# Relative attention of layer 1: scores as 64-row by 32-column tiles read straight from the projected keys, with four banks for scores and values and turn-back sharing two

## The chip, the cores and the metric

The kernel runs on 1 core of one Trainium2 chip. It is a whole vision-transformer tower in one program: 64 images, 26 tokens each (one class token and a 5 by 5 grid), width 192, four layers. The metric is the device time of one execution in microseconds (us); lower is better. All arithmetic is fp32; the large products are split into high and low fp32r parts, the small ones (scores, values) are plain fp32 matmuls, and the profiler records such a plain fp32 matmul as two MATMUL and two LDWEIGHTS instructions.

Engines are named as in the profile: PE is TensorE's matmul side, PEld its weight loads (which overlap PE), DVE is VectorE, ACT ScalarE, POOL GpSimd, SP SyncE.

## The reference, cut to what matters

Only the attention of layer 1 is touched. For every image, with 12 heads of 64 features:

```
qkv = (x @ qkv_w.T).reshape(b, n, 3, HEADS, HEAD_DIM).transpose(2, 0, 3, 1, 4)
q, k, v = (qkv[0], qkv[1], qkv[2])
attn = jnp.einsum('bhqd,bhkd->bhqk', q, k) * scale
r_p_k = tab_kv[iv] + tab_kh[ih]
attn = attn + jnp.einsum('bhqd,qkd->bhqk', q, r_p_k) * scale
attn = jax.nn.softmax(attn, axis=-1)
out = jnp.einsum('bhqk,bhkd->bhqd', attn, v)
r_p_v = tab_vv[iv] + tab_vh[ih]
out = out + jnp.einsum('bhqk,qkd->bhqd', attn, r_p_v)
out = out.transpose(0, 2, 1, 3).reshape(b, n, QKV_DIM)
return out @ proj_w.T + proj_b
```

`iv` and `ih` are the row and column distances of two tokens in the grid (a fixed index for the class token), so the relative parts are small products with tables of 10 rows each.

## The kernel before, in words

`attention(cfg, ...)` is one function for all attentions of the tower. For layer 1, `cfg.kind` is "rel", `G` is 2 and `NC` is 6: the 64 images are worked in 8 turns (`i` = 0 to 7) of 8 images, 208 tokens; each turn has two tiles (`g` = 0, 1; tile number `t` = 2i + g) of four images, each image in 32 partitions. q and k are projected transposed, six chunks each of 128 partitions (two heads of 64 features) by 208 tokens.

What runs in a turn is written out by hand as `order` (for PE and ACT) and `dve_order` (for DVE), lists of steps with the number of turns they run ahead: on PE k of the next turn, relative mass of tile 0 (`mass`), q of the next turn, `scores` 0 of the next turn, `values` 0, projection of v, `scores` 1, output projection of the turn before (`out`), mass 1, values 1, v, and turning the result back (`back`). The engines are held together by counting semaphores alone; each runs its list in order.

- Keys. ACT copies a projected chunk of k from PSUM to `k_t` (L1975). The chunk holds two heads one above the other, so `spread` (L2168 to L2179) has DVE multiply each chunk by a 0/1 mask per head into `k_x` (L2177), 12 instructions a turn, and raises `k_done`.
- Scores (`scores`, L1744). For tile t, 6 chunks by 4 images make 24 matmuls (L1775) of 128 rows by 32 stationary columns (the queries) and 52 moving columns (the masked keys of two heads), all into one bank, `bank[4 + g]`. PE waits for `s_used` (that tile t - 2 has been read), and on tile 0 of a turn for `k_done` and for the last copy of q. Behind them come 24 matmuls with the tables of the keys (`rel_scores`, L1785); ACT copies that result to `rel` (L2021), and DVE's `shift` starts with it (L2237, L2243), adds the scores (L2251, L2252), subtracts the maximum; ACT takes the exponential (L2028), DVE's `normalise` divides, sums the relative mass (L2290) and transposes the probabilities (L2299).
- Values (`values`, L1799). 48 recorded matmuls from the probabilities and v (L1806) and from the mass and the tables (L1832), into one of three banks 0 to 2 in turn; ACT copies them out (L2052, `av_used`).
- Back (`add_back`, L1898 and L2334). The output is turned back in pieces of 128 tokens (one or two a turn) into bank 3, by two transposes a piece (L1907, L1908); DVE adds each to the residual (L2338), and PE waits for that before the next piece. The five turns 1, 3, 4, 6 and 7 have two pieces.
- Banks 6 and 7 serve all other results in turn (`job`).

Of the kernel before, what the change touches and what calls it, by code (L numbers as in the profile page):

```python
# [18 lines left out]
ALU = mybir.AluOpType  # L19
# [81 lines left out]
def vit_tower(nc, a, out, stop=99):  # L101
# [12 lines left out]
    with ctx:  # L114
# [1340 lines left out]
        def attention(cfg, res, *others, stats_too=True):  # L1455
# [14 lines left out]
            rel_kind = cfg.kind == "rel"  # L1470

            kq = {"performer": [("fk", 0, 1)]}.get(cfg.kind, [("k", 0, 1), ("q", 0, 1)])
# [30 lines left out]
            else:  # L1503
# [33 lines left out]
            def added_back(i, g):  # L1537
# [7 lines left out]
            NA, NB = len(av_banks), len(back_banks)  # L1545

            def back_at(y, tiles):

                return bank[2][:, D * (y - tiles[0]):D * (y - tiles[0]) + D] if tiled else bank[back_banks[y % NB]]

# [4 lines left out]

            def score_banks():

                return psum[:, 3 * 512:6 * 512].rearrange("p (r x) -> p r x", r=3)[:, :, 0:NC * pairs * SLOT]

# [173 lines left out]
            def tensor(pe):  # L1733
# [10 lines left out]
                def scores(i, g):  # L1744
                    t = G * i + g
                    pe.wait_ge(s_free.sem, s_free_at + t - (0 if tiled else 1))
                    if g == 0 and cfg.kind == "causal" and i == 0:
                        keep_clock(bank[4], 8)
                    if cfg.mix and t == 0:
                        pe.wait_ge(mix["scores"], 1)  # L1750
                    if g == 0:
                        pe.wait_ge(s["k_done"].sem, b["k_done"] + i + 1)
                        used(last_qk[0], i, last_qk[1])
                    if tiled:
                        for c in range(NC):
                            kx = key_rows(i, c * pairs, pairs).rearrange("p (u n) -> p u n", n=n)
# [42 lines left out]
                def values(t, g):  # L1799
# [8 lines left out]
                    for v in range(halves):  # L1808

                        unit = halves * t + v  # L1810
                        pe.wait_ge(s["av_used"].sem, b["av_used"] + unit - NA + 1)
                        ob = bank[av_banks[unit % NA]]
                        if no == 2:
                            low_heads = H * 2 // 3
                            for c in range(2):
                                for y in range(in_cell):
                                    for strip in range(4):
                                        h = in_cell * strip + y if c == 0 else low_heads + in_cell * (strip % 2) + y
                                        ins = product(ob[:, 104 * c:104 * c + 104], h, strip, y == 0, y == in_cell - 1)
                        else:  # L1820
                            if v == 0:
                                pe.wait_ge(s["rel_table"].sem, b["rel_table"] + 5)
                                used("mass", t, 0)
                            for k in range(3):
                                c, p = divmod(3 * v + k, 2)
# [3 lines left out]
                                part = rel_mass[g][:, 128 * c:128 * c + 128].rearrange("p (b s) -> p b s", s=32)  # L1829
                                for u in range(2):  # L1830
                                    r0 = 128 * p + 64 * u
                                    ins = nc.tensor.matmul(o[64 * u:64 * u + 64, :], rel_table[:, r0:r0 + 64],  # L1832
                                                           part[:, :, 0:SLOT], start=False, stop=True)
# [64 lines left out]
                def add_back(i, g):  # L1898
                    used("out", i, 1)
                    ident = shp[:, SHAPE_COLS["ident"]]  # L1900
                    tiles = added_back(i, g)
                    for y in tiles:

# [42 lines left out]
            def scalar(act):  # L1946
# [7 lines left out]
                def projections(i, ys):  # L1954

                    if cfg.kind == "causal" and i:

                        act.wait_ge(s["qk_ready"].sem, b["qk_ready"] + 4 * (i - 1) + parts.index(ys) + 1)
                    elif cfg.kind != "performer":
                        act.wait_ge(s["k_done"].sem, b["k_done"] + i)  # L1960
# [59 lines left out]
                def rel_scores(t, g):  # L2020
                    nc.scalar.activation(rel[g][:, :, :].rearrange("p h r -> p (h r)"),  # L2021
                                         job("rel", t, 0)[:, 0:240], ACT.Identity)\
                        .then_inc(s["job_used"].sem, 1)
# [7 lines left out]
                def values(i, g):  # L2031
# [9 lines left out]
                    for v in range(halves):  # L2041
                        act.wait_ge(s["av_full"].sem, b["av_full"] + halves * t + v + 1)
                        src = bank[av_banks[(halves * t + v) % NA]][:, 0:104 * m].rearrange("p (c n) -> p c n", c=m)
                        dst = o4[:, v * m:v * m + m, g, :]
# [52 lines left out]
            def vector(dve):  # L2097
# [90 lines left out]
                def shift(t, g):  # L2188
# [3 lines left out]
                    if tiled:  # L2192
                        n4 = [128, 3, NC * pairs, SLOT]
                        sc = score_banks().rearrange("p r (h s) -> p r h s", s=SLOT)
                        z_as, mx_as = z.rearrange("p (r h) s -> p r h s", r=3), mx.rearrange("p (r h) -> p r h", r=3)
                        spread_out = mx_as.unsqueeze(3).to_broadcast(n4)
# [30 lines left out]
                    if cfg.kind == "rel":  # L2227
# [19 lines left out]
                        z4 = z[:, :, 1:SLOT].rearrange("p h (a c) -> p h a c", c=5)  # L2247
                        s4 = sc[:, :, 1:SLOT].rearrange("p h (a c) -> p h a c", c=5)
                        m0 = m12[:, 2, :].unsqueeze(2)
                        link(nc.vector.tensor_tensor(m0, rl[:, :, 0:1], rl[:, :, 10:11], ALU.add))  # L2250
                        nc.vector.tensor_tensor(z[:, :, 0:1], sc[:, :, 0:1], m0, ALU.add)  # L2251
# [5 lines left out]
                        src = z  # L2257
                    link(nc.vector.tensor_reduce(mx_as, src, AX.X, ALU.max))
# [113 lines left out]
            for name, uses in (("s_used", cfg.kind != "softmax"), ("z_full", cfg.kind in ("softmax", "rel", "causal")),  # L2372
                               ("p_full", cfg.kind != "performer"),
                               ("qk_ready", cfg.kind in ("performer", "causal"))):
                if not uses:
# [351 lines left out]
```

## Time and profile before

| | |
|---|---|
| time before, median of 3 runs | 2929.98 us (2927.67 to 2931.74) |
| the profiled execution | 2936.78 us, its span 2935.0 us |
| PE busy in the span | 2697.6 us, 92% |
| DVE busy | 2054.5 us, 70% |
| ACT busy | 1051.7 us, 36% |
| mean granted TensorE clock | 0.944 of full speed |
| the layer-1 attention | about 1645 to 1897 us of the span |

The shares are means over a program of very different stages; the layer-1 attention is under 9% of it. "idle before, releaser" tells how long an engine stood before an instruction and which instruction of another engine ended that; "issue" is a wait for nothing that the profile shows.

### The profile page before, as it was taken

How to read it: one execution, taken by the hardware profiler on the slowest of the kernel's cores; microseconds unless marked ns; L12 is line 12 of the kernel's file. 1: busy time of each engine (PE TensorE's matmuls, PEld its weight loads, DVE VectorE, ACT ScalarE, POOL GpSimd, SP SyncE). 2: the span in 40 equal slices, each digit the busy share in tenths (PEclk: the TensorE clock that was granted, in tenths of full speed). 3: DMA queues.
4: the chain of work that ended last, by engine and by line, in shares of the span. 5: the costliest groups of instructions: out<-in, count | busy, mean ns of one | idle time of the engine just before them, and what ended most of it. 6: DMA issues, size and time to landing. Idle time of an engine off the chain costs nothing. (4 is left out here: it accounts for less than half of the span.)

```text
span 2935.0 us, 61848 instructions
## 1 busy us (share of the span) xinstructions
PE 2697.6 (92%) x22697; PEld 2457.8 (84%) x22697; DVE 2054.5 (70%) x5173; ACT 1051.7 (36%) x2050; POOL 655.3 (22%) x820
## 2 busy tenths in 40 slices
PE   8889999999999999999999788799797889967788
PEld 7679999999999999999999678767466789956567
DVE  3857777777777767777777788723567676778877
ACT  2433332333333333323333444411355443324533
POOL 1312122122122121221221211021223211113561
PEclk9979999999999999999999899979898889979888
DMA  3001011010010110110100000057100100000000
GB/s 144 25 35 39 20 38 38 19 38 31 26 38 19 38 38 19 38 38 19 38 19 32 9 2 2 7 175 227 34 2 2 58 20 20 1 27 3 25 20 18
DMA packets 24481, 105.91 MB, mean 36 GB/s; under 512 B 4455, under 2 KB 9463, under 8 KB 19086
## 3 DMA queue, kind: packets, MB, share of 16 engines
q1 hardware_dynamic: 22654, 99.62, 9.9%
q0 software_dynamic: 1584, 3.30, 0.3%
q8 instruction: 121, 1.98, 0.3%
q14 instruction: 122, 1.00, 0.1%
HBM read 98.32 MB, written 6.64 MB: 36 GB/s over the span
## 5 line engine op out<-in xcount | busy, mean ns | idle before, releaser
L919 ACT ACTIVATE hid<-psum,dat 128x384 f32<-128x384 f32 (+1 forms) x912 | 555.2, 610 | 1143.1 <-PE psum L603 1027.4
L884 PE MATMUL psum<-w,hid_hi 128*128 128x384 f32 x2964 | 858.7, 361 | 2.2 <-DVE y_tok L935 1.6
L886 PE MATMUL psum<-w,hid_lo 128*128 128x192 f32 x2964 | 745.6, 252 | 0.0
L886 PEld LDWEIGHTS psum<-w,hid_lo 128*128 128x128 f32 x2964 | 570.9, 193 | 1.7
L884 PEld LDWEIGHTS psum<-w,hid_hi 128*128 128x128 f32 x2964 | 561.4, 189 | 5.7 <-issue 4.1
L953 DVE TENSOR_TENSOR hid_lo<-hid,hid_hi 128x384 fp32r<-128x384 f32 (+1 forms) x912 | 539.9, 592 | 31.5
L950 DVE CAST hid_hi<-hid 128x384 fp32r<-128x384 f32 (+1 forms) x912 | 340.9, 374 | 122.0 <-ACT hid L919 120.5
L976 DVE SCALAR_TENSOR_TENSOR h_tok<-psum,gate,h_tok 128x192 f32<-128x192 f32 x416 | 173.4, 417 | 248.3 <-PE psum L886 244.8
L603 PE MATMUL psum<-xa_hi,w_hi 128*128 128x384 f32 (+1 forms) x912 | 324.2, 356 | 0.6 <-DVE xb L556 0.4
L603 PE MATMUL psum<-xa_lo,w_hi 128*128 128x384 f32 (+1 forms) x912 | 322.7, 354 | 0.0
L603 PE MATMUL psum<-xb,w_lo 128*128 128x384 f32 (+1 forms) x912 | 322.0, 353 | 0.0
L603 PE MATMUL psum<-xa_hi,w_lo 128*128 128x384 f32 (+1 forms) x912 | 321.4, 352 | 0.0
L603 PE MATMUL psum<-xb,w_hi 128*128 128x384 f32 (+1 forms) x912 | 319.8, 351 | 0.0
L778 POOL TENSOR_TENSOR w_lo<-raw,w_hi 128x1536 fp32r<-128x1536 f32 x38 | 132.8, 3496 | 676.4 <-DVE hid_lo L953 676.4
L773 POOL CAST w_hi<-raw 128x1536 fp32r<-128x1536 f32 x38 | 55.8, 1467 | 625.5 <-DVE hid_lo L953 589.6
L1708 POOL COPY n_tok<-p_x 32x312 f32<-32x312 f32 (+1 forms) x192 | 94.5, 492 | 446.8 <-DVE p_x L2299 270.7
L982 DVE SCALAR_TENSOR_TENSOR h_tok<-psum,gate,h_tok 128x192 f32<-128x192 f32 x416 | 173.7, 418 | 14.2
L603 PEld LDWEIGHTS psum<-xa_hi,w_hi 128*128 128x128 f32 x912 | 172.2, 189 | 11.4 <-issue 1.5
L603 PEld LDWEIGHTS psum<-xb,w_hi 128*128 128x128 f32 x912 | 172.4, 189 | 10.6
L603 PEld LDWEIGHTS psum<-xa_hi,w_lo 128*128 128x128 f32 x912 | 172.3, 189 | 9.9
L603 PEld LDWEIGHTS psum<-xb,w_lo 128*128 128x128 f32 x912 | 172.1, 189 | 9.8
L603 PEld LDWEIGHTS psum<-xa_lo,w_hi 128*128 128x128 f32 x912 | 172.7, 189 | 8.5
(363 smaller groups left out, 4233.2 us busy)
## 6 DMA issues: line engine op xcount, KB each, us to landing
raw<-in_L_exp SPq DMA_DIRECT2D x36, 1344.0 KB, 5.8
w_e<-in_L_exp SPq DMA_DIRECT2D x20, 576.0 KB, 3.9
w_e<-in_L_exp SPq DMA_DIRECT2D x20, 384.0 KB
pix<-in_pixels SPq DMA_DIRECT2D x6, 832.0 KB, 10.4
w_e<-in_L_exp SPq DMA_DIRECT2D x20, 195.0 KB
raw<-in_L_mlp SPq DMA_DIRECT2D x2, 1344.0 KB, 5.7
wp_raw<-in_L_att SPq DMA_DIRECT2D x1, 2304.0 KB, 8.4
route_rows<-in_rows_clear SPq DMA_DIRECT2D x1, 2000.0 KB, 23.3
```

Source lines behind the costliest of these rows:

```text
L603: ins = nc.tensor.matmul(o, l, r, start=start and n == 0, stop=stop and n == 4)
L773: nc.gpsimd.tensor_copy(w1_hi[j][:, :, :], r1).then_inc(s["w_split"].sem, 1)
L778: nc.gpsimd.tensor_tensor(w1_lo[j][:, :, :], r1, w1_hi[j][:, :, :].bitcast(F32), ALU.subtract).then_inc(s["w_split"].sem, 1)
L884: nc.tensor.matmul(o[:, 0:2 * D], hid_hi[k % 2][:, m, c], w2[j][:, m, :], start=m == 0, stop=False)
L886: ins = nc.tensor.matmul(o[:, 0:D], hid_lo[k % 2][:, m, c], w2[j][:, m, 0:D], start=False, stop=m == HC - 1)
L919: nc.scalar.activation(hid[(6 * k + m) % 3][:, 0:128 * nt], bank[4 + (6 * k + m) % 4][:, 0:128 * nt], func, bias=bias).then_inc(s["h_act"] ...
L950: nc.vector.tensor_copy(hid_hi[k % 2][:, m, 0:w], h).then_inc(s["dve_step"].sem, 1)
L953: nc.vector.tensor_tensor(hid_lo[k % 2][:, m, 0:w], h, hid_hi[k % 2][:, m, 0:w].bitcast(F32), ALU.subtract).then_inc(s["h_split"].sem, 1)
L976: nc.vector.scalar_tensor_tensor(res[:, t, :], o[:, 0:D], g, res[:, t, :], ALU.mult, ALU.add).then_inc(s["dve_step"].sem, 1)
L982: nc.vector.scalar_tensor_tensor(res[:, t, :], o[:, D:2 * D], g, res[:, t, :], ALU.mult, ALU.add).then_inc(s["y_used"].sem, 1)
L1708: nc.gpsimd.tensor_copy(p_bd[t % 2][r, :, SLOT * im:SLOT * im + SLOT], p_x[t % 2][r, 0:H, 0:SLOT]).then_inc(s["bd_low"].sem, 1)
```

## The change

The rel kind now takes the path that the other attentions of the tower use for scores in array tiles.

- `spread` is gone from DVE's list, and nobody waits for `k_done` in this attention.
- Scores are 6 chunks by 4 images by 2 heads, 48 matmuls of 64 rows by 32 stationary columns and 26 moving columns, straight from `k_t`. The upper 64 rows (one head of each chunk) write one bank, the lower 64 another: banks 2 and 3 for tile 0, banks 4 and 5 for tile 1.
- The heads therefore stand in another order (even heads first); ACT's copy of `rel` writes that order, values read it through `place`, and DVE adds the scores in two instructions of 6 heads where there was one of 12.
- Values have banks 0 and 1 instead of 0, 1 and 2. Turning back shares bank 0: both pieces of a turn are written side by side, DVE is told of both at once, and PE has a wait for `av_used` ahead of them and one for `t_used` ahead of values 0.

```diff
+                dve_order = [step for step in dve_order if step[0] != "spread"]
...
-            tiled = cfg.kind in ("softmax", "log2", "causal")
-            pairs = 32 // d if tiled else 0
-            av_banks, back_banks = ((0, 1, 2), (3,)) if G == 2 else ((0, 1), (2,) if tiled else (2, 3))
+            tiled, features_wide = cfg.kind != "performer", False
+            strips, first_strip = (4, 2) if features_wide else (3, 3)
+            if rel_kind:
+                strips, first_strip = 2, 2
+            deep = 128 // strips if rel_kind else 32
+            pairs = 1 if features_wide or rel_kind else 32 // d if tiled else 0
+            av_banks, back_banks = ((0, 1), (0,)) if G == 2 else ((0, 1), (2,) if tiled else (2, 3))
...
                     if g == 0:
-                        pe.wait_ge(s["k_done"].sem, b["k_done"] + i + 1)
+                        if not (features_wide or rel_kind):
+                            pe.wait_ge(s["k_done"].sem, b["k_done"] + i + 1)
                         used(last_qk[0], i, last_qk[1])
...
-                                for r in range(3):
-                                    rows, x = slice(32 * r, 32 * r + 32), c * w
-                                    ins = nc.tensor.matmul(bank[3 + r][32 * im:32 * im + 32, x:x + w],
+                                for r in range(strips):
+                                    rows, x = slice(deep * r, deep * r + deep), c * w
+                                    ins = nc.tensor.matmul(bank[first_strip + r + (2 * (g % 2) if rel_kind else 0)][32 * im:32 * im + 32, x:x + w],
                                                            q_t[rows, q0:q0 + 32], kx[rows, :, m:m + SLOT],
                                                            start=True, stop=True)
...
+                        if rel_kind and g == 0 and v == 0 and t >= 2 * G:
+
+                            pe.wait_ge(s["t_used"].sem, b["t_used"] + added_back(t // G - 2, 0)[-1] + 1)
...
+                    if rel_kind:
+
+                        pe.wait_ge(s["av_used"].sem, b["av_used"] + halves * min(G * (i + 2), G * NI) - 1)
                     for y in tiles:
...
-                        nc.vector.tensor_tensor(z4, s4, rel_u[:, 0, :, :].unsqueeze(3).to_broadcast(g4),
-                                                ALU.add).then_inc(s["s_used"].sem, 1)
+                        for r in range(2):
+                            hs = slice(6 * r, 6 * r + 6)
+                            s4 = sc[:, r, :, 1:SLOT].rearrange("p h (a c) -> p h a c", c=5)
+                            ins = nc.vector.tensor_tensor(z4[:, hs], s4, rel_u[:, 0, hs, :].unsqueeze(3).to_broadcast([128, 6, 5, 5]),
+                                                          ALU.add)
+                        ins.then_inc(s["s_used"].sem, 1)
```

PE's instructions from the end of q of turn 1 into values 0, before (q_t and k_x are queries and masked keys, dat the tables; a row of this list is a matmul as the program writes it):

```order
1904 L603 MATMUL psum<-xb,wp_lo 128x208
1905 L1775 MATMUL psum<-k_x,q_t 32x52 [waits job_used,k_done,s_used]
1906 L1775 MATMUL psum<-k_x,q_t 32x52 x23
1907 L1785 MATMUL psum<-dat,q_t 32x40 [waits job_used]
1908 L1785 MATMUL psum<-dat,q_t 32x40 x23
1909 L1806 MATMUL psum<-n_tok,v_x 64x104 [waits av_used,rel_table,bd_low,job_used,bd_full]
```

and now:

```order
1904 L603 MATMUL psum<-xb,wp_lo 128x208
1905 L1773 MATMUL psum<-k_t,q_t 32x26 [waits job_used,s_used]
1906 L1773 MATMUL psum<-k_t,q_t 32x26 x47
1907 L1795 MATMUL psum<-dat,q_t 32x40 [waits job_used]
1908 L1795 MATMUL psum<-dat,q_t 32x40 x23
1909 L1816 MATMUL psum<-n_tok,v_x 64x104 [waits av_used,rel_table,bd_low,job_used,bd_full]
```

Twice as many score matmuls of half the width stand in the same place, one wait fewer ahead of them; nothing else moves on PE.

PE where a turn's two pieces are turned back, between v and k, before (feat is the transposed result):

```order
2276 L603 MATMUL psum<-wp_lo,xs 128x384
2277 L1907 MATMUL psum<-shp,feat 128x128 [waits t_used,job_used]
2278 L1908 MATMUL psum<-shp,feat 128x128
2279 L1907 MATMUL psum<-shp,feat 128x128 [waits t_used]
2280 L1908 MATMUL psum<-shp,feat 128x128
2281 L603 MATMUL psum<-xa_hi,wp_hi 128x208 [waits lo_full,job_used]
```

and now:

```order
2276 L603 MATMUL psum<-wp_lo,xs 128x384
2277 L1929 MATMUL psum<-shp,feat 128x128 [waits t_used,av_used,job_used]
2278 L1930 MATMUL psum<-shp,feat 128x128
2279 L1929 MATMUL psum<-shp,feat 128x128 [waits t_used]
2280 L1930 MATMUL psum<-shp,feat 128x128
2281 L603 MATMUL psum<-xa_hi,wp_hi 128x208 [waits lo_full,job_used]
```

The first piece has the new wait for `av_used`. The second one's wait for `t_used` is for the same count as the first one's now, not for the add of the first piece.

## Rows read from the trace of the kernel before

**Rows 1.** Page, part 1: engine, busy us, share of the span, instructions.

```profile
PE 2697.6 (92%) x22697; PEld 2457.8 (84%) x22697; DVE 2054.5 (70%) x5173; ACT 1051.7 (36%) x2050; POOL 655.3 (22%) x820
```

**Rows 2.** Windows (stretch, length, busy us by engine, clock, DMA): whole attention, one turn.

```profile
1645.00:1895.00 250.00, 206.91 (x3302) 188.97 (x3302) 208.46 (x739) 103.34 (x256) 46.09 (x94) 0.95 0.01 2
1838.57:1866.49 27.92, 24.62 (x415) 22.37 (x415) 25.26 (x91) 12.88 (x33) 5.03 (x10) 1.00 0.01 3
```

**Rows 3.** Waits of PE, 1645 to 1895 us: who waited for whom, us, times, longest.

```profile
PE psum L1806 <- ACT k_x L2017: 14.5, 9, 1.9
...
PE psum L603 <- ACT k_x L2017: 4.2, 7, 0.6
PE psum L1775 <- ACT q_t L1975: 4.2, 8, 0.5
...
PE psum L1892 <- DVE o_lo L2325: 2.7, 1, 2.7
PE psum L1907 <- DVE h_tok L2338: 1.8, 4, 0.5
```

**Rows 4.** Waits of DVE in the same stretch.

```profile
DVE rel_u L2237 <- ACT rel L2021: 20.6, 13, 5.3
```

**Rows 5.** Groups on DVE, same stretch: shapes xcount, busy us, mean ns, idle before.

```profile
L2177 DVE TENSOR_SCALAR k_x<-k_t,shp 128x208 f32<-128x208 f32 x96 | 26.0, 340 | 2.5 <-ACT k_t L1975 2.3
...
L2252 DVE TENSOR_TENSOR z_t<-psum,rel_u 128x300 f32<-128x300 f32 x16 | 7.4, 460 | 0.0
L2251 DVE TENSOR_TENSOR z_t<-psum,m 128x12 f32<-128x12 f32 x16 | 2.9, 182 | 0.6
```

**Rows 6.** Timeline at scores 0 (start us, length us, engine; rows*columns of array tile).

```profile
1769.06 0.76 PE L1775 MATMUL psum<-k_x,q_t 128*32 128x52 f32 x48 [0.53 <-ACT q_t L1975]
...
1769.61 0.67 PE L1785 MATMUL psum<-dat,q_t 128*32 128x40 f32 x48
```

**Rows 7.** Timeline of PE in layer 0's attention (scores in 32*32 tiles).

```profile
76.97 0.61 PE L1763 MATMUL psum<-k_x,q_t 32*32 32x26 f32 x48
77.51 0.43 PE L603 MATMUL psum<-xa_hi,wp_hi 128*96 128x416 f32 x1
```

**Rows 8.** Timeline of PE in a layer-2 attention: scores, then values.

```profile
2251.16 0.68 PE L1763 MATMUL psum<-k_x,q_t 32*32 32x52 f32 x48
2251.77 0.92 PE L1806 MATMUL psum<-n_tok,v_x 128*32 128x104 f32 x32
```

**Rows 9.** Timeline of PE: its stops with no releaser, behind scores 0.

```profile
1685.51 0.31 PE L1832 MATMUL psum<-k_x 128*64 128x104 f32 x2 [1.71 <-issue]
...
1712.40 0.25 PE L1806 MATMUL psum<-n_tok,v_x 128*64 128x104 f32 x1 [1.69 <-issue]
...
1740.35 0.75 PE L1785 MATMUL psum<-dat,q_t 128*32 128x40 f32 x36 [1.39 <-issue]
...
1799.44 0.40 PE L1806 MATMUL psum<-n_tok,v_x 128*64 128x104 f32 x4 [1.47 <-issue]
```

**Rows 10.** Page, part 3: the queue that brings instructions.

```profile
q8 instruction: 121, 1.98, 0.3%
```

**Rows 11.** Timeline of turning back two pieces, PE and DVE.

```profile
1758.22 0.27 PE L1907 MATMUL psum<-shp,feat 128*128 128x128 f32 x1
...
1758.64 0.36 DVE L2338 TENSOR_TENSOR h_tok<-psum,h_tok 128x192 f32<-128x192 f32 x1
1759.05 0.33 PE L1907 MATMUL psum<-shp,feat 128*128 128x128 f32 x1 [0.45 <-DVE h_tok L2338]
...
1759.53 0.36 DVE L2338 TENSOR_TENSOR h_tok<-psum,h_tok 128x192 f32<-128x192 f32 x1 [0.53 <-PE psum L1908]
...
1896.86 0.36 DVE L2338 TENSOR_TENSOR h_tok<-psum,h_tok 128x192 f32<-128x192 f32 x1 [0.53 <-PE psum L1908]
```

**Rows 12.** Timeline at the start of the attention: DVE, then PE.

```profile
1659.83 0.42 DVE L2237 TENSOR_SCALAR rel_u<-rel,shp 128x60 f32<-128x60 f32 x2 [5.27 <-ACT rel L2021]
...
1670.03 0.51 PE L603 MATMUL psum<-xa_hi,wp_hi 128*128 128x208 f32 x1 [5.01 <-issue]
```

More of the change, by code:

```diff
@@ L1541, in added_back, with av_bank @@
                 return range(first, middle) if g == 0 else range(middle, end)
-            tiled = cfg.kind in ("softmax", "log2", "causal")
-            pairs = 32 // d if tiled else 0
-            av_banks, back_banks = ((0, 1, 2), (3,)) if G == 2 else ((0, 1), (2,) if tiled else (2, 3))
+            tiled, features_wide = cfg.kind != "performer", False
[5 more added lines that the diff above has]
+            av_banks, back_banks = ((0, 1), (0,)) if G == 2 else ((0, 1), (2,) if tiled else (2, 3))
             NA, NB = len(av_banks), len(back_banks)
+            def av_bank(unit):
+                return bank[(0, 1, 1, 1)[unit % 4]] if features_wide else bank[av_banks[unit % NA]]
             def back_at(y, tiles):
-                return bank[2][:, D * (y - tiles[0]):D * (y - tiles[0]) + D] if tiled else bank[back_banks[y % NB]]
+                return bank[back_banks[0]][:, D * (y - tiles[0]):D * (y - tiles[0]) + D] if tiled else bank[back_banks[y % NB]]
             def place(h):
@@ L1554, in place, with score_banks @@
                 return (x // pairs * NC + c) * pairs + x % pairs if tiled else h
-            def score_banks():
-                return psum[:, 3 * 512:6 * 512].rearrange("p (r x) -> p r x", r=3)[:, :, 0:NC * pairs * SLOT]
+            def score_banks(g):
+                first = first_strip + 2 * (g % 2) if rel_kind else first_strip
+                return psum[:, first * 512:(first + strips) * 512].rearrange("p (r x) -> p r x", r=strips)[:, :, 0:NC * pairs * SLOT]
             C = cfg.dve_steps
@@ L1745, in scores @@
                     t = G * i + g
-                    pe.wait_ge(s_free.sem, s_free_at + t - (0 if tiled else 1))
+                    pe.wait_ge(s_free.sem, s_free_at + t - (1 if rel_kind or not tiled else 0))
                     if g == 0 and cfg.kind == "causal" and i == 0:
@@ L1810, in values @@
                         unit = halves * t + v
-                        pe.wait_ge(s["av_used"].sem, b["av_used"] + unit - NA + 1)
-                        ob = bank[av_banks[unit % NA]]
+                        pe.wait_ge(s["av_used"].sem, b["av_used"] + (unit - (3, 1, 0, 0)[g] if features_wide else unit - NA + 1))
+                        if features_wide and g == 0 and t >= 2 * G:
+                            pe.wait_ge(s["t_used"].sem, b["t_used"] + added_back(t // G - 2, 1)[-1] + 1)
+                        if rel_kind and g == 0 and v == 0 and t >= 2 * G:
+                            pe.wait_ge(s["t_used"].sem, b["t_used"] + added_back(t // G - 2, 0)[-1] + 1)
+                        ob = av_bank(unit)
                         if no == 2:
@@ L1824, in values @@
                             for k in range(3):
-                                c, p = divmod(3 * v + k, 2)
                                 o = ob[:, 104 * k:104 * k + 104]
@@ L1828, in values @@
                                     product(o, 2 * (3 * v + k) + u, u, True, False)
-                                part = rel_mass[g][:, 128 * c:128 * c + 128].rearrange("p (b s) -> p b s", s=32)
                                 for u in range(2):
-                                    r0 = 128 * p + 64 * u
+                                    c, p = divmod(place(2 * (3 * v + k) + u), 4)
+                                    part = rel_mass[g][:, 128 * c:128 * c + 128].rearrange("p (b s) -> p b s", s=32)
+                                    r0 = 64 * p
                                     ins = nc.tensor.matmul(o[64 * u:64 * u + 64, :], rel_table[:, r0:r0 + 64],
@@ L1901, in add_back @@
                     tiles = added_back(i, g)
+                    if features_wide and g == 0:
+                        pe.wait_ge(s["av_used"].sem, b["av_used"] + min(G * (i + 1) + 1, G * NI))
+                    if rel_kind:
+                        pe.wait_ge(s["av_used"].sem, b["av_used"] + halves * min(G * (i + 2), G * NI) - 1)
                     for y in tiles:
@@ L1958, in projections @@
                         act.wait_ge(s["qk_ready"].sem, b["qk_ready"] + 4 * (i - 1) + parts.index(ys) + 1)
-                    elif cfg.kind != "performer":
+                    elif cfg.kind not in ("performer", "rel"):
                         act.wait_ge(s["k_done"].sem, b["k_done"] + i)
@@ L2020, in rel_scores @@
                 def rel_scores(t, g):
-                    nc.scalar.activation(rel[g][:, :, :].rearrange("p h r -> p (h r)"),
-                                         job("rel", t, 0)[:, 0:240], ACT.Identity)\
+                    nc.scalar.activation(rel[g][:, :, :].rearrange("p (u c) r -> p c u r", u=2),
+                                         job("rel", t, 0)[:, 0:240].rearrange("p (c u r) -> p c u r", u=2, r=20), ACT.Identity)\
                         .then_inc(s["job_used"].sem, 1)
@@ L2042, in values @@
                         act.wait_ge(s["av_full"].sem, b["av_full"] + halves * t + v + 1)
-                        src = bank[av_banks[(halves * t + v) % NA]][:, 0:104 * m].rearrange("p (c n) -> p c n", c=m)
+                        src = av_bank(halves * t + v)[:, 0:104 * m].rearrange("p (c n) -> p c n", c=m)
                         dst = o4[:, v * m:v * m + m, g, :]
@@ L2192, in shift @@
                     if tiled:
-                        n4 = [128, 3, NC * pairs, SLOT]
-                        sc = score_banks().rearrange("p r (h s) -> p r h s", s=SLOT)
-                        z_as, mx_as = z.rearrange("p (r h) s -> p r h s", r=3), mx.rearrange("p (r h) -> p r h", r=3)
+                        n4 = [128, strips, NC * pairs, SLOT]
+                        sc = score_banks(g).rearrange("p r (h s) -> p r h s", s=SLOT)
+                        z_as, mx_as = z.rearrange("p (r h) s -> p r h s", r=strips), mx.rearrange("p (r h) -> p r h", r=strips)
                         spread_out = mx_as.unsqueeze(3).to_broadcast(n4)
@@ L2247, in shift @@
                         z4 = z[:, :, 1:SLOT].rearrange("p h (a c) -> p h a c", c=5)
-                        s4 = sc[:, :, 1:SLOT].rearrange("p h (a c) -> p h a c", c=5)
                         m0 = m12[:, 2, :].unsqueeze(2)
                         link(nc.vector.tensor_tensor(m0, rl[:, :, 0:1], rl[:, :, 10:11], ALU.add))
-                        nc.vector.tensor_tensor(z[:, :, 0:1], sc[:, :, 0:1], m0, ALU.add)
-                        nc.vector.tensor_tensor(z4, s4, rel_u[:, 0, :, :].unsqueeze(3).to_broadcast(g4),
-                                                ALU.add).then_inc(s["s_used"].sem, 1)
+                        nc.vector.tensor_tensor(z_as[:, :, :, 0], sc[:, :, :, 0], m0.rearrange("p (r h) s -> p r (h s)", r=2),
+                                                ALU.add)
[3 more added lines that the diff above has]
+                            ins = nc.vector.tensor_tensor(z4[:, hs], s4, rel_u[:, 0, hs, :].unsqueeze(3).to_broadcast([128, 6, 5, 5]),
+                                                          ALU.add)
+                        ins.then_inc(s["s_used"].sem, 1)
                         dve.wait_ge(s["s_used"].sem, b["s_used"] + t + 1)
@@ L2373, in attention @@
                                ("p_full", cfg.kind != "performer"),
-                               ("qk_ready", cfg.kind in ("performer", "causal"))):
+                               ("qk_ready", cfg.kind in ("performer", "causal")), ("k_done", not rel_kind)):
                 if not uses:
```

4 lines of the change are left out of this document (2 added, 2 removed).

## The prediction, made before the changed kernel was run

> **What bounds the kernel now.** I started from the page's busy shares [rows 1], which say only that PE is busiest over the whole program, and went to the one stage that the change touches. In windows [rows 2], the stage from 1645 to 1895 us has PE busy for 206.9 us and DVE for 208.5 of 250; in a quiet turn of 27.92 us it is 24.6 and 25.3. Two engines stand level, so shares decide nothing, and I read the waits in both directions. DVE waits 20.6 us, in 13 places, for ACT's copy of the relative scores [rows 4], which ACT makes as soon as PE has them: DVE waits for PE in every turn. PE waits for DVE only in two places [rows 3]: 4 times 0.45 us for the add of a first piece turned back, and once 2.7 us at the very end for the last split. Its other waits are for ACT's copies of PE's own results: 0.53 us eight times before scores 0, 0.60 us in q behind the mass copy, and up to 1.9 us before values 1. They have the same length turn after turn, whatever DVE did. So PE with its round trips over ACT sets the length of a turn. In no turn does PE wait for the spread keys: ahead of scores 0 it waits for the copy of q [rows 6].
>
> One place is bound by DVE: at the start, DVE gets its first relative scores at 1659.83 and PE then stands 5.01 us until 1670.03, behind ACT, which comes to v only after the exponentials of DVE's two tiles [rows 12]. No spread lies in that stretch.
>
> **Spread removed.** 96 instructions, 26.0 us busy [rows 5], 3.25 us a turn. All of it lies beside PE's work, and DVE already waits for PE behind it, so DVE will wait longer and I cost it at zero. If my reading were wrong and DVE were the bound, it would be worth most of its 26 us; that is a rival. The wait for `k_done` goes with it, and it was never the late one of its three.
>
> **Scores.** Each tile issues 48 recorded matmuls of 52 columns now and 96 of 26 columns after. Before: 0.76 us less the 0.21 that one takes, over 47 steps, is 11.7 ns a step, and the table matmuls start 0.55 us after the first [rows 6]. For 26 columns the nearest row is layer 0's, in tiles of 32 by 32: 0.61 less 0.19 over 47 is 9.0 ns [rows 7]. Halving the columns there gains little: with 52 columns in such tiles a step takes (0.68 - 0.20)/47 = 10.2 ns [rows 8]. A tile of 64 rows was never run. I take 9.0 ns: 96 steps are 0.86 us, 0.31 more than now, and for 16 tiles +4.9 us. Bounds: 11.7 ns, as now, gives 1.12 - 0.55 = 0.57 a tile, +9.2 us; I see nothing that would issue faster than 9.0, but allow 8.5 ns, +4.3 us. Nothing hides it: scores stand in PE's own chain and the q wait comes before them.
>
> **A change of tile shape.** Scores and table matmuls use the same shape now (128 by 32), and the second follows the first without a gap: the last score starts 47 steps behind 1769.06, at 1769.61, where the table group starts [rows 6]. Between different shapes there is one: layer 0's last score starts at 76.97 + 0.42 = 77.39 and the projection at 77.51, 0.12 us [rows 7]. The change puts such a border behind every tile's scores (64 by 32, then 128 by 32): 16 x 0.12 = +1.9 us; from 0 to +3.2 us (0.2 each). The Trainium skill, TensorEngine Tiling (Array Packing), Key Properties, says that a change of tiling mode drains the engine; the trace agrees with 0.12 us, and without this rule one would leave the term out.
>
> **Stops with no releaser.** PE stands four times for 1.39 to 1.71 us, 6.3 us in all, with nothing to wait for, each time in the dense small matmuls behind scores 0 [rows 9]. Counting PE's recorded instructions (loads, matmuls, semaphore instructions) between these stops gives 768, 768 and 1792: 3, 3 and 7 times 256. The queue that brings instructions moved 1.98 MB in 121 packets, 16.4 KB each [rows 10]. I read the stops as arrivals at a new block of instructions that is not there yet. Counted from the first score of tile 0 they come at instruction 205, 202, 121 and 211; block borders at 126, 36 and 41 passed without a stop, and behind scores 1, borders at 65 to 155 did too. So the exposed stretch began near 121 and reached at least 19 instructions past the two dense groups (192 instructions). The Trainium skill, Runtime: NRT & Kernel Launch, Instruction fetch mechanics, has blocks of 16 KiB, 256 instructions, and calls the crossing mostly hidden; by that I would cost this at nothing, but the trace shows 1.57 us at four of the crossings.
>
> After the change the dense groups are 288 long, and the attention has 1541 more PE instructions, so six more borders. Placing them by the new order, counted on from the same start, six scores 0 have a border inside the widened stretch (at 260, 271, 294, 276, 254 and 232, turns 0, 1, 4, 5, 6, 7), two just past it (333, 316), and two scores 1 have one further in than has passed freely (181, 163). At four in five of the six, and one or two of the others, I take seven stops where there were four: 3 x 1.57 = +4.7 us. Ends: two fewer (-3 us) to eleven (+11 us).
>
> **Turning back.** With both pieces written before DVE adds, PE no longer stands 0.45 us between them [rows 11]. Three of the five turns with two pieces lie in PE's chain (turns 1, 3, 4): -1.35 us. The other two are at the end, where DVE's adds are in the chain; each has a 0.53 us wait of DVE for the second piece, of which two transposes at 0.11 us come back: about -0.85 for both. Together -2.2 us; at worst 0, if ACT's copies take up the slack at the start of k. The new wait for `av_used` is for ACT's copy of values 1's first half, made over 2 us earlier, behind a whole v projection; queued behind it would be k, and I cost it at nothing, at most 0.2 us a turn. Values never need the third bank: the unit two back was copied before.
>
> **DVE's split add.** A 128x300 add from PSUM takes 460 ns and a 128x12 one 182 [rows 5]; on that line a 128x150 takes 315, and two overlapping by 0.09 us are about 0.1 to 0.17 us longer. It is beside PE except for three tiles (both at the start, one at the end): +0.4 us.
>
> **Sum.** 4.9 + 1.9 + 4.7 - 2.2 + 0.4 = +9.7 us, against the profiled execution's 2936.78 us (span 2935.0 and 1.8 around it). That execution lies 6.8 us above the median of the runs, so I add the sum to the median: 2929.98 + 9.7 = 2939.7 us, slower by 0.33%.
>
> **Rivals.** (a) The stops don't grow: borders fall in harmless places or the fetch runs ahead. Then 4.9 + 1.9 - 2.2 + 0.4 = +5.0 us, 2935.0, within the 0.2% (5.9 us) that a measurement of this kernel can tell. For it: the stops came at only four of some 27 borders; against: where a border fell deep behind scores 0 it cost in four of five. (b) DVE is the bound after all, because ACT's list ties its copies to DVE's exponentials, and PE's even waits are DVE's in disguise. Then the turns shrink by the spread less the split add, 8 x (3.25 - 0.3) = 23.6 us, less until PE becomes the bound: PE stands some 3 us a turn (27.92 - 24.62), and with the scores' growth only about 20 us remain: 2910. For it: DVE is busy 25.3 of 27.9; against: DVE's waits for PE in every turn, and that the list of waits has PE waiting for DVE for 4.5 us in all. (c) Matmuls of 26 columns in 64-row tiles issue far slower, as ones of 104 columns do: (0.92 - 0.27)/31 = 21 ns [rows 8], 2.0 us a tile instead of 0.55, +23 us in place of +4.9: 2958. Against it: layer 0's 9.0 ns. The Trainium skill, TensorEngine Tiling, Instruction Overhead, gives about 60 cycles a matmul whatever its columns; 48 more matmuls at an estimated 25 ns would be +19 us and some 2954; the trace's 9.0 and 11.7 ns speak against the rule.
>
> **Chances.** The forecast with more stops 0.58, of it one in ten within 0.2%; (a) 0.25, one in five of it above the bound and one in five faster than 0.2% below because some other gain exists; (b) 0.12; (c) 0.05. That is slower by over 0.2% 0.62, within 0.2% 0.21, faster 0.17. The sum's bounds reach from -1 (4.3 + 0 - 3 - 2.2 + 0.2) to +23 us (9.2 + 3.2 + 11 - 1 + 0.6), hardly all at one end; 2926 to 2952 leaves out (b), (c) and the far end.
>
> **What would show it.** Right: every turn without a stop at about 28.3 us (27.92 + 2 x 0.43 - 0.45; the 27.92 holds one wait between pieces), DVE busy about 22.3 us of it and its waits for `rel` grown by some 3 us a turn; scores' first start to the tables' first start 0.9 to 1.0 us; some seven stops with no releaser in the dense groups; no wait of PE for h_tok between pieces. Wrong: turns near 25 us with PE no longer waiting the same 1.6 and 0.6 us for ACT (b); a step of over 12 ns in the scores (c); four stops or fewer (a); or a new wait of PE for ACT's o_f copy before turning back.

## The result and the profile after

The changed kernel takes 2948.29 us (median of 4 runs, 2946.47 to 2950.64) against 2928.82 us for the kernel before in the same comparison: a ratio of 1.0061, 95% interval 1.0048 to 1.0074, slower by 0.61%. The forecast was 2939.7, slower by 0.33%, with a range of 2926 to 2952. The sign was right; the loss is about twice the sum, and most of the difference lies in the clock and in the number and length of the stops.

The first part of the profile's page, after, and the line of its third on the queue that brings instructions:

```profile
PE 2696.8 (92%) x23465; PEld 2459.3 (84%) x23465; DVE 2028.5 (69%) x5093; ACT 1051.5 (36%) x2050; POOL 653.3 (22%) x820
q8 instruction: 127, 2.08, 0.3%
```

DVE does 26 us less than in [rows 1], PE has 768 more matmuls in the same busy time, and the instruction queue moves 127 packets where [rows 10] had 121. Neither share says why the program is longer. For that I measured the attention itself, from the load of its first score to the point where PE begins to drain at the end of its list: 238.41 us before, 255.10 after, +16.7 us. (That point stands at the second of the last two pieces turned back before and at the first one after, which makes the loss look up to 0.5 us smaller than it is.) The rest of the program was 7 us shorter in the profiled run of after than in that of before, which had been 6.8 us above its median. So nearly all of the loss is in this stage.

Windows over the same 150 us of the stage, before first, then after (stretch, length, busy us by engine, granted clock, DMA share, GB/s):

```profile
1700.00:1850.00 150.00, 129.24 (x2103) 117.63 (x2103) 134.35 (x478) 67.97 (x170) 28.29 (x55) 0.99 0.01 2
```

```profile
1700.00:1850.00 150.00, 127.22 (x2516) 116.79 (x2517) 109.81 (x395) 62.29 (x155) 24.42 (x50) 0.95 0.01 2
```

ACT, whose work in a turn is the same, gets through 155 instructions instead of 170: after makes less progress here, PE is idle 2 us more, and its granted clock is lower.

The waits of PE over the stage after (who waited for whom, us in total, times, longest), which answer to [rows 3]:

```profile
PE psum L1816 <- ACT k_x L2039: 14.4, 9, 1.9
PE psum L1795 <- issue: 10.8, 5, 2.6
...
PE psum L603 <- ACT k_x L2039: 4.2, 7, 0.6
PE psum L1773 <- ACT q_t L1997: 4.2, 8, 0.5
PE psum L1816 <- issue: 4.0, 3, 2.0
PE psum L1908 <- DVE o_lo L2351: 2.9, 1, 2.9
```

The waits for ACT have the same sizes as before (14.4, 4.2 and 4.2 us against 14.5, 4.2 and 4.2). The waits for `h_tok` are gone. What grew is "issue", a stop for which the profile names no releaser. DVE, the same view, against [rows 4]:

```profile
DVE rel_u L2259 <- ACT rel L2043: 67.8, 15, 15.0
```

20.6 us of waiting have become 67.8: DVE handed its spread to its own idle time, and then waited for PE's stops as well. The stops themselves, in the timeline of PE (start, length, idle before):

```profile
1655.47 0.35 PE L1795 MATMUL psum<-dat,q_t 128*32 128x40 f32 x15 [1.86 <-issue]
...
1681.59 0.42 PE L1795 MATMUL psum<-dat,q_t 128*32 128x40 f32 x10 [2.01 <-issue]
...
1768.78 0.40 PE L1816 MATMUL psum<-n_tok,v_x 128*64 128x104 f32 x4 [2.03 <-issue]
...
1800.19 0.36 PE L1795 MATMUL psum<-dat,q_t 128*32 128x40 f32 x7 [2.09 <-issue]
...
1832.19 0.54 PE L1795 MATMUL psum<-dat,q_t 128*32 128x40 f32 x17 [2.58 <-issue]
...
1864.74 0.74 PE L1795 MATMUL psum<-dat,q_t 128*32 128x40 f32 x28 [2.22 <-issue]
```

These are six of eight; two more are of 0.87 and 1.06 us. Every one of the eight turns has one, in or just behind scores 0. Together they are 14.7 us, against 6.3 us in [rows 9] and 0.56 in a smaller one.

What follows can be slow too. Values 0 of one turn behind the stop at 1768.78, and values 1 of another, the same 48 matmuls in shape:

```profile
1768.78:1772.73 3.95, 3.95 (x49) 3.74 (x48) 3.14 (x12) 0.43 (x1) 0.00 (x0) 0.57 0.02 4
1846.92:1849.20 2.28, 2.28 (x48) 2.16 (x48) 2.11 (x8) 0.78 (x2) 0.00 (x0) 1.00 0.03 7
```

They take 3.95 us at a granted clock of 0.57 (nearly all of it at the lower level, 1.2 GHz) and 2.28 us at 1.00 (2.4 GHz). Ahead of the slow one PE had stood 0.53 us for q and 2.03 us in the stop. Ahead of the fast one it had stood too, for ACT's copy of `k_x`:

```profile
1846.92 0.40 PE L1816 MATMUL psum<-n_tok,v_x 128*64 128x104 f32 x4 [1.62 <-ACT k_x L2039]
```

Nor does every stop come with a lower clock. In after it is lower during or behind the six stops of 1.86 to 2.58 us and stays up at those of 0.87 and 1.06. In before it is lower behind the stops of 1.71 and 1.39 us, and stays up behind those of 1.69 and 1.47, though PE had stood 0.53 us for q shortly ahead of each of these two. Here are the 3 us behind the one of 1.69:

```profile
1712.40:1715.40 3.00, 3.00 (x50) 2.86 (x50) 3.00 (x14) 0.86 (x2) 1.37 (x4) 1.00 0.03 5
```

Stretches at the lower level add up to some 20.5 us of the stage before and some 37.5 us after.

### The profile page after: what moved, and what is told of

Same layout as the page of the kernel before. It is cut to its first block and busy times, and to the rows that moved or that the text cites. A ratio compares the mean times of both kernels' runs of the same rounds, so it can differ in the third digit from the quotient of the medians.

```text
span 2944.6 us, 63288 instructions
## 1 busy us (share of the span) xinstructions
PE 2696.8 (92%) x23465; PEld 2459.3 (84%) x23465; DVE 2028.5 (69%) x5093; ACT 1051.5 (36%) x2050; POOL 653.3 (22%) x820
## 5 line engine op out<-in xcount | busy, mean ns | idle before, releaser
L603 PEld LDWEIGHTS psum<-xb,w_hi 128*128 128x128 f32 x912 | 172.3, 189 | 10.6
```

The source lines that it names most:

```text
L603: ins = nc.tensor.matmul(o, l, r, start=start and n == 0, stop=stop and n == 4)
```

## The experiments

Times are medians of 4 to 12 runs; "the stage" is measured as above, from the first score to PE's drain. The kernel before had 2931.58 us in the first four comparisons and 2929.79 in the last four; after is 19.5 us above before.

**spread_kept.** The change, with DVE's spread of the keys still made; nobody reads it, and only ACT's copies of the next keys wait for it:

```
- dve_order = [step for step in dve_order if step[0] != "spread"]
- elif cfg.kind not in ("performer", "rel"):
+ elif cfg.kind != "performer":
  (and DVE's loop over the heads, its masks and the signal k_done as before)
```

> The changed kernel, with DVE still spreading the keys into k_x (12 instructions a turn, 26 us of DVE in all) though nobody reads them; only ACT's copy of the next keys waits for them. If PE with its round trips over ACT sets the turns, DVE's relief was worth nothing: the time is that of the changed kernel, 2948 us within 3. If DVE is near enough to the bound that its relief already pays inside the change, this run is slower than the changed kernel by 5 to 20 us, and PE shows waits for DVE again.

Measured: 2950.30 us, 1.0069 (1.0056 to 1.0082). In place of 67.8 us DVE waits 39.5 us for `rel`:

```profile
DVE rel_u L2258 <- ACT rel L2042: 39.5, 14, 8.5
```

The stage takes 254.86 us against 255.10. Taking 26 us of work off DVE is worth nothing that these runs can tell, as forecast; the rival in which DVE is the bound falls.

**back_alone.** The kernel before with only the turning back changed:

```
- ... if tiled else bank[back_banks[y % NB]]
+ ... if tiled or rel_kind else bank[back_banks[y % NB]]
  (and the same condition at PE's wait, its increments and DVE's wait)
```

> The kernel before, with only the turning back changed: both pieces of a turn side by side in bank 3, DVE told of both at once; scores, spread and three value banks as before. By the two traces three turns lose 0.68 us each on PE and the end about 1 to 1.4: 3 to 3.5 us faster than before, 2925.5. If the start of k is paced by ACT's copies of v all the same, the gain is under 1 us.

Measured: 2924.96 us, 0.9983 (0.9974 to 0.9992), a gain of 6.6 us by the medians and 5.0 by the ratio; the stage from its first score is 231.90 us, 6.5 less than before. That is twice what was expected, and the trace accounts for both halves. About 3.3 us are at the turning back itself. The rest is at the end of the stage, in the last output projection: before, then back_alone.

```profile
1887.60:1895.40 7.80, 7.37 (x36) 7.19 (x36) 3.54 (x22) 0.83 (x2) 0.00 (x0) 0.58 0.01 2
```

```profile
1877.90:1885.00 7.10, 4.27 (x36) 4.09 (x36) 6.27 (x26) 0.48 (x2) 0.00 (x0) 1.00 0.01 3
```

The same 36 matmuls are busy 7.37 us at 0.58 and 4.27 us at 1.00. In after this projection runs at 0.60 again, so that the change as a whole doesn't get these 3 us. Why the clock stays up in back_alone isn't settled: the waits ahead of it differ by parts of a us.

**one_by_one.** The change, with the pieces turned back one by one as before:

```
- ... if tiled else bank[back_banks[y % NB]]
+ ... if tiled and not rel_kind else bank[back_banks[y % NB]]
  (and the same at the waits and increments)
```

> The changed kernel, with the pieces of a turn turned back one by one as before (PE waits for DVE's add of the first before it writes the second). Turning back alone gave 6.6 us in the kernel before, twice what I expected. If the parts of the change add up, this run is slower than the changed kernel by 5 to 7 us, 2954; if the gain was that of moved borders or of chance there, 3 to 3.5 us, 2951.5. The growth of the score tiles with their stops would then be the whole of the loss: 2954 - 2931 = 23 us.

Measured: 2954.00 us, 1.0092 (1.0073 to 1.0112), 5.7 us above after by the medians. The intervals of the two touch; the stage has the same sign, 257.56 us from its first score, 2.5 more than after. The 2954 that was expected came out, but partly by luck: of the 6.3 us by which its profiled span is longer, 2.5 are in the stage and 0.9 just ahead of it, and 3 us are elsewhere in the program, where the edit changes nothing. PE's waits between pieces are back:

```profile
PE psum L1929 <- DVE h_tok L2364: 2.3, 5, 0.5
```

From both sides turning back two pieces together gains: 6.5 us of the stage on the old scores, 2.5 on the new ones, where the last projection runs slow anyway.

**borders_moved.** The change, with 200 semaphore increments on PE ahead of the stage, so that the borders of 256 instructions fall elsewhere:

```
+ for _ in range(200 if rel_kind else 0):
+     hold(pe)
```

> The changed kernel, with 200 increments of an unused semaphore in PE's list at the start of this attention, where PE stands several us for POOL anyway. Theory of instruction blocks: every border of 256 PE instructions then falls 200 instructions earlier against the scores, so that the eight stops behind scores 0 (now at instruction 260, 271, 333, 316, 294, 276, 254, 232 from the first score) move to 60, 71, 133, 116, 94, 76, 54, 32 and to 256 behind these; the ones under 116 vanish, and of the eight stops (14.7 us) and the half clock behind them two to four short ones are left, in all 10 to 18 us faster than the changed kernel, near 2933. Rival: the stops belong to the dense small matmuls themselves or to the change of tile shape, wherever the borders lie; then eight stops stay and the time is 2948 within 3.

Measured: 2967.81 us, 1.0122 (1.0105 to 1.0139): slower, not faster. The waits of PE:

```profile
PE psum L603 <- issue: 35.3, 3, 31.1
```

By their own records the 200 increments run from 1637.53 to 1668.24 us, 154 ns each. They cover the 5.8 us that PE waits for POOL there in after, and the first score comes some 26 us later: the edit costs more than what it tests. Read from the first score on, the stage takes 249.07 us, 6.0 less than after. The borders that now stand at instruction 33 to 92, counted from a tile's first score, pass freely, but the next border, 256 further on (289 to 348), now falls in values 0, and PE stops there (0.9 to 2.5 us). So there are eight stops again, 13.7 us against 14.7: the stops moved with the borders, as the theory has it, but there are as many as in after, where the expectation had two to four.

**borders_moved_2.** The same shift with 50 tiny matmuls, whose 200 recorded instructions are quick:

```
+ if rel_kind and name == "q" and i == 0:
+     for _ in range(50):
+         nc.tensor.matmul(bank[5][0:32, 0:SLOT], shp[0:32, 0:32], shp[0:32, 0:SLOT], ...)
```

> The changed kernel, with 50 tiny matmuls (200 PE instructions, under 1 us) into a free bank between k and q of turn 0, in place of the 200 semaphore increments that cost some 25 us at the front in the run before. Borders fall as in that run: behind scores 0 a border at 59, 69, 75, 92, 54 passes freely but drags one at 325, 331, 348, 310 with it, since dense scores and tables (288 instructions) are longer than a block; 113 and 130 stop. In that run the stretch from the first score to the end of the stage took 249.1 us against 255.1. Theory of blocks: the same here, so 5 to 6 us faster than the changed kernel, 2943. Rival (the stretch was shorter for another reason, such as the long stand before it): 2948 within 3.

Measured: 2944.17 us, 1.0045 (1.0032 to 1.0059). The stops of PE in it:

```profile
PE psum L1816 <- issue: 5.4, 3, 2.4
PE psum L1773 <- issue: 4.2, 2, 2.6
PE psum L1848 <- issue: 2.1, 2, 1.4
PE psum L1795 <- issue: 1.8, 1, 1.8
```

They have moved from the tables (`L1795`, 10.8 us after) to scores and values. With no edit to the stage's work but its place among the borders, the stage from its first score on is 248.20 us instead of 255.10, as expected. But the stops are eight again and 13.5 us in all, only 1.2 less than after. What changed more is the time at the lower clock level, 27.3 us of the stage instead of 37.5. At the ratio of the two groups of values above (3.95 and 2.28 us) 10.2 us less of it would be worth an estimated 4.3 us, so that most of the gain would be the clock's. Ahead of it the padding costs some 3 us (from the drain to the first score 21.9 us, 18.8 after). In all kernels every stop in the dense matmuls falls at the same remainder of PE's recorded instruction count by 256. So the stops are at the borders, and their price depends on what stands there, 0 to 3 us. In the changed order a border behind scores 0 stopped PE from about 113 to 348 instructions behind the first score, nearly 256, so that a shift mostly trades one border inside for the next.

**values_first.** The change, with values 0 ahead of scores 0, so that the dense stretch is no longer scores, tables and values in one piece behind the wait for q:

```
- ("q", 0, 1), ("scores", 0, 1), ("values", 0, 0), ("v", 0, 1)
+ ("q", 0, 1), ("values", 0, 0), ("scores", 0, 1), ("v", 0, 1)
```

> The changed kernel, with values 0 moved ahead of scores 0 of the next turn in the order of PE and ACT. My theory: PE no longer stands 0.53 us for the copy of q before scores 0 (values fill it), and the sequencer has plain work queued when it comes to the dense scores, as it has before scores 1, where no stop was seen; DVE gets its relative scores 2.3 us later but has over 5 us to spare in a turn now. So 8 x 0.5 = 4 us from the wait and up to 15 us from the stops: 2930 to 2938. Rival: DVE becomes late (its wait for rel lies in front of the longest chain) and PE waits for px; then 2945 or more. Second rival: the stops stay, since the blocks are fetched no earlier: 2944.

Measured: 2928.60 us, 0.9993 (0.9984 to 1.0002), 19.7 us below after and no different from before. Its window over the same stretch, and its waits of PE:

```profile
1700.00:1850.00 150.00, 135.99 (x2786) 124.79 (x2786) 116.83 (x420) 69.78 (x175) 28.72 (x60) 1.00 0.01 3
```

```profile
PE psum L1795 <- issue: 2.8, 2, 2.2
PE psum L1773 <- issue: 1.8, 5, 0.5
PE psum L1773 <- ACT q_t L1997: 0.5, 1, 0.5
```

The clock is 1.00 where after has 0.95, and PE is idle for 14.0 of the 150 us instead of 22.8. The stage is 233.89 us from its first score, 21.2 less than after. The stops together are 4.6 us instead of 14.7 (-10.1), the wait for q is 0.5 instead of 4.2 (-3.7), which values 0 now cover, and some 7 us are left, for which the clock at its upper level is the likely cause: 17.1 us of the stage are at the lower level instead of 37.5. No run separates a stop from the slow stretch behind it.

The new order also moves the borders against the scores, by some 100 instructions in every turn but the first, and one could put the gain down to that. The trace speaks against it: seven borders now stand 134 to 231 instructions behind the first score of scores 0, where the old order had stopped at 113 and at 130, and only the one at 231 stops PE (0.58 us). The first scores 0 of the stage have no values ahead of them, and their border at 259 still costs 2.18 us. Small stops of 0.1 to 0.5 us have come up in scores 1, where after has none.

**values_first_spread.** values_first with the spread kept, edits as above.

> The changed kernel with values 0 ahead of scores 0, and DVE spreading the keys as before, read by nobody. It asks whether DVE's relief is worth something once PE is faster. Turns of 27.3 us there, DVE busy 22.4: with the spread 25.4, and DVE may not start on a tile's scores until PE has them, 2.3 us later in the turn than before. If DVE becomes the bound: 5 to 20 us slower than values_first (2928.6), that is 2934 to 2948; if it still hides, 2929 within 3. I lean to the first.

Measured: 2930.17 us, 1.0002 (0.9993 to 1.0011), 1.6 us above values_first. I had leaned to a price for the spread once PE's stops were gone. DVE has its work back and still waits for PE:

```profile
1700.00:1850.00 150.00, 135.75 (x2628) 124.34 (x2626) 136.51 (x495) 70.18 (x177) 27.69 (x55) 1.00 0.01 3
```

```profile
DVE rel_u L2258 <- ACT rel L2042: 22.2, 9, 8.1
```

DVE is busy for 136.51 of 150 us, and of its 49.1 us of waits in values_first 22.2 are left. The stage takes 234.57 us against 233.89. A share of 91% was not yet a bound.

**old_scores_values_first.** back_alone with the same change of order: the old scores (128 by 32, 52 columns, keys spread).

> The kernel before (128-row scores, spread keys, three value banks) with both pieces turned back at once and values 0 ahead of scores 0. If values first hides the stops and the wait for q there too and DVE hides behind PE, this is the fastest: 2925.0 less 8 x 0.53 less up to four stops of 1.6 us, 2914 to 2921. If DVE with its spread becomes the bound, as its 25.3 us of a 27 us turn let one fear, the gain is lost: 2925 or more, and the array tiles would have their use.

Measured: 2920.02 us, 0.9968 (0.9956 to 0.9980), 28 us below after and the fastest of all. Its stage is 226.04 us from the first score, and its waits of PE are small:

```profile
PE psum L1794 <- DVE p_x L2299: 1.8, 1, 1.8
PE psum L1785 <- issue: 1.3, 4, 0.5
PE psum L1775 <- ACT q_t L1975: 0.5, 1, 0.5
```

Against values_first it has the old scores, with the spread and the three value banks that belong to them, and is 8.6 us faster by the medians, 7.3 by the ratios (the stage 7.85 us). Some 3.3 us of that are stops (4.6 us in values_first, 1.3 here); the rest goes to the new scores themselves.

## Why the prediction was right in sign and short in size

**Spread: right.** Cost at zero; spread_kept is 2.0 us from after and values_first_spread 1.6 us from values_first, both within what the comparisons can tell, and DVE's waits took up the difference.

**Scores and the tile shape: right in mechanism, the sum near.** The first scores of a tile, after:

```profile
1765.16 1.00 PE L1773 MATMUL psum<-k_t,q_t 64*32 64x26 f32 x96 [0.53 <-ACT q_t L1997]
...
1766.10 0.66 PE L1795 MATMUL psum<-dat,q_t 128*32 128x40 f32 x48
```

(1.00 - 0.19) over 95 is 8.5 ns a step, just under the forecast 9.0 and at the lower end of the bound. From first score to first table it is 0.94 us, where the forecast had 0.9 to 1.0. The last score starts at 1765.97, and the tables 0.13 us behind it: the drain at a change of tile shape, 0.12 us in the forecast. From first score to first table all sixteen tiles take 15.2 us against 9.7, of which 0.6 are a small stop; without it that is +6.0 for the 6.8 of the two terms. The Trainium skill, TensorEngine Tiling (Array Packing), Instruction Overhead, has about 60 cycles a matmul, an estimated 25 ns; the trace has 8.5 ns a recorded matmul and 17 a matmul of the program, both below it.

**Stops: right in place, short in number and length.** This is the first of the two steps of the sum that failed. The working placed six borders inside the widened stretch and two just past it, and counted seven stops. In the trace the borders came within three instructions of where it put them (259, 269, 330, 313, 292, 275, 254 and 233), and all eight stopped. The term took 1.57 us each, from tiles half as long; the eight are 0.87 to 2.58, mean 1.84. Before had 6.8 us, the four of [rows 9] and a fifth one of 0.56 us at a border 46 instructions into scores 1 of turn 0, which the working had overlooked. So the growth was 7.9 us, not 4.7. The borders at 313 and 330, beyond the 288 of the dense groups, stopped too (1.06 and 0.87 us): the exposed stretch reaches into values 0. The borders behind scores 1, at 81 to 206, all passed freely, against my one or two.

**The clock: missing from the sum.** This is the second step that failed. Scores and shape, stops and turning back make 6.0 + 7.9 - 3.3 = 10.6 of the stage's 16.7 us; some 6 us are left. They agree with the 17 us more at the lower level (3.95 us for values that take 2.28 makes them worth an estimated 7 us). The turn from 1796.58 to 1828.18 us shows it in small: of its 31.60 us the forecast's 28.3 for a turn without a stop and the 2.09 of its stop leave 1.2, and its values 0 ran at the lower level. No run forced the clock alone; borders_moved_2, with nearly the same sum of stops and 10 us less at the lower level, comes nearest. So this part is read from the traces and not shown by itself. I had read each stop of [rows 9] as its own length; behind most of the long ones the price was what followed too. Before, that was there already: the values behind its stop of 1.39 us have a row of the same kind, here beside the same group of a turn without a stop.

```profile
1741.03:1744.70 3.67, 3.67 (x51) 3.56 (x48) 2.92 (x15) 0.80 (x2) 0.54 (x3) 0.60 0.02 4
...
1854.85:1857.10 2.25, 2.25 (x48) 2.16 (x48) 1.69 (x8) 0.79 (x2) 1.61 (x5) 1.00 0.00 0
```

Had I compared these two in the profile of before, a further stop would have been worth 1.57 us and up to 1.4 more, the latter behind two of the four.

**Turning back: right in mechanism, gain too small.** -2.2 forecast, -2.8 in the trace: 0.67 us in each of three turns and 0.41 in each of the last two. In the stage as measured here it is -3.3, since its end stands at the first of the last pieces. The experiments have 2.5 and 6.5, the latter with 3 us of the last projection. Two pieces, after, against [rows 11]:

```profile
1818.08 0.27 PE L1929 MATMUL psum<-shp,feat 128*128 128x128 f32 x1
...
1818.41 0.27 PE L1930 MATMUL psum<-shp,feat 128*128 128x128 f32 x1
...
1818.72 0.62 DVE L2364 TENSOR_TENSOR h_tok<-psum,h_tok 128x192 f32<-128x192 f32 x2 [0.33 <-PE psum L1930]
```

Four transposes follow each other at 0.11 us; the three two-piece turns in PE's chain gain 0.67 us each, not 0.45, as the second piece's own start is saved too.

**DVE's split add: smaller still.** 32 adds of 303 ns stand where 16 of 460 were, and since two overlap they are busy 8.4 us against 7.4, 0.06 us more a tile, where the forecast had 0.1 to 0.17:

```profile
L2277 DVE TENSOR_TENSOR z_t<-psum,rel_u 128x150 f32<-128x150 f32 x32 | 8.4, 303 | 0.0
```

**The rivals.** (a), stops that don't grow, fell with eight for five. (b), DVE as the bound, fell with spread_kept and values_first_spread. (c), slow issue, fell with 8.5 ns. The 2954 that went with 60 cycles a matmul lies nearer to the result (2948.3) than the forecast does, but by luck: the scores cost 6 us of the 19 that it had for them.

## What to carry to other kernels

A stop that the profile ascribes to nothing may have a price beyond its own length: compare the same group of instructions behind it and elsewhere, at both granted clocks, and put that into the sum. Where an engine's instruction count changes, count the borders of its instruction blocks again, and see what stands at each; an order with the one dense run split in two, and its wait covered, was worth 20 us here, more than the change had cost. Relief for an engine that already waits was worth nothing that could be told here, even where the engine was busy for 91% of the stretch.

## What the runs showed of the hardware that was not expected

- At every 256th recorded instruction PE stands or passes freely, by what stands there and what ran ahead of it. The eight in the dense stretch behind scores 0 cost 0.87 to 2.58 us in after; those behind scores 1 cost nothing. The Trainium skill, Runtime: NRT & Kernel Launch, Instruction fetch mechanics, calls the crossing mostly hidden; in values_first, where the stops are 4.6 us for the whole stage, that nearly holds, in after, with 14.7 us, it doesn't. Why values ahead of scores hides them isn't settled: no run here removed the wait for q alone.
- A semaphore increment takes PE about 154 ns: 200 of them, 30.7 us (borders_moved); 50 tiny matmuls, 200 recorded instructions too, some 3 us.
- 64-row by 32-column tiles with 26 columns pass at 8.5 ns a step, 128-row tiles with 52 at 11.7.
- Behind some stops PE had the lower clock for the next microseconds, and 48 matmuls of values cost 1.4 to 1.7 us more. The lower clock came at all six stops of 1.86 to 2.58 us in after and at two of four of 1.39 to 1.71 us in before (1.71 and 1.39, not 1.69 and 1.47); it did not come behind a single wait of 1.62 us.
- The last projection's clock (0.58 before, 1.00 in back_alone) is worth 3 us. What decided which it was isn't settled.
